# One scratch layout, one load for a part, new places, x in pieces and gram on 128 tokens in a convolution, FFT and MLP kernel

## The chip, the cores and the metric

The kernel runs on one core of a Trainium2 chip. The metric is the device time of one execution in microseconds (us), the median of several. A core has TensorE (PE, matrix products), VectorE (DVE), ScalarE (ACT), GpSimd (POOL) and SyncE (SP, which issues nearly all DMA transfers here), each with an instruction stream of its own. They meet at semaphores only. Sixteen DMA engines move data between HBM and the on-chip memory (SBUF, 128 partitions).

## The reference

`x` has the shape (32, 96, 56, 56): 32 images, 96 channels, 3,136 positions. Layer 0 is a ternary inverted residual block with batch statistics, layer 1 a token mixer with an FFT over the positions and an MLP with 8-bit operands:

```python
# layer 0; planes = 576
out = relu(batchnorm(conv(x, ternarize(w1)), g1, b1))
out = relu(batchnorm(conv(out, ternarize(w2), stride=1, pad=1, groups=planes), g2, b2))
out = batchnorm(conv(out, ternarize(w3)), g3, b3)
x = out + x
# layer 1; t is x as (image, position, channel)
t = t + attn(_ln_t(t)); t = t + ffn(_ln_t(t))

def attn(x):
    h = relu(_bn(einsum('bnc,hc->bnh', x, w1), ...))        # 192 hidden
    X = fft(h, axis=1, norm='ortho')
    xr = relu(X.real * rd - X.imag * idg + rb)
    xi = relu(X.imag * rd + X.real * idg + ib)
    y = ifft(xr + 1j * xi, axis=1, norm='ortho').real
    return _bn(einsum('bnh,ch->bnc', y, w2), ...)
def ffn(x):                                                 # fp8e5 operands, 384 hidden
    return _qlinear(relu(_qlinear(x, W1, b1)), W2, b2)
```

The mean and variance of the first batchnorm are over all images and positions, so nothing of the second convolution can start before all of `x` has been read once.

## The kernel before, in words

The program has four stages, one behind the other.

**Gram** (about 12 to 264 us). The statistics of the first batchnorm come from the products of `x` with itself over the positions. SP loads one image a transfer into one of two buffers (`xa`, L435). TensorE transposes blocks of `TP` = 112 positions (L458), ScalarE copies four of them from PSUM to `xT` (L494), and TensorE multiplies each by itself and sums into `gps` (L464): 28 blocks an image, in 7 groups of 4. Four transposes of one group and four products of the group before alternate.

**Convolution** (280 to 1880 us). `conv_sync`, `conv1_tensor` and their like run 16 image pairs, each with 18 steps `v` (two images, nine slices of channels). TensorE makes the 1x1 convolution (L651) and the depthwise one as products with diagonal taps (L683). SP stores four pieces of the result `z` a step (L618). At `v` = 1 and 8 it loads a whole image of the next pair into `xin` (L629), 96 partitions x 3,136; ScalarE and GpSimd split it into two 16-bit parts (`xhi_scalar`, L192, and L201).

**Projection** (1880 to 2553 us). `z` comes back in eighths of a pair, is normalised, and is multiplied by the third weight (L966). The result goes to `z_scratch` in halves (`store_half`). SP's part of it ends with a wait for the last stores.

**Tokens** (2553 to 5093 us). `tokens_stage` is a software pipeline over 32 images. A table `PLACES` gives each step one or more places on a line; `NT` = 2000 places are one turn, and a step placed at s belongs to turn position s mod 2000 for the image that started s div 2000 turns earlier. So up to `LAGS` = 5 images are in work, and each engine issues in the order of the places. There is no other order: an engine that waits holds all that stands behind it in its stream. The steps of one image:
- `load_in` (L1229, L1230) brings chunk c of the layer-0 result (`zin`) and of `x` (`x_tok`), seven chunks of 448 positions in three buffers; `act_bn3` (L1617) and `pool_y` (L1661) add them to `y`, `store_t` keeps a copy. With chunks 3 and 6 of image 0 the tables `t1c`, `g2c`, `g3c`, `t4c` are loaded (`load_tables`).
- `mean1` (L1336), `square1` (L1342) give the statistics of the first layer norm; a load `y<-va` (L1252) puts a row of `y` back.
- `w1` (L1474) and `stage1` (L1485) are the first linear map and the first stage of the FFT. `act_a` (L1605) writes a seventh of the result `a`, 128 partitions x 768, and `store_a` (L1287) stores it: seven stores an image, on the semaphores `st_a[p]`.
- `load_b` (L1263) brings the same data back the other way round as `bt`: 112 partitions (4 x 28) by frequency k, in four parts of 8, 8, 8 and 5 frequencies, each part with four transfers. The first part waits for all seven stores.
- `spectrum` (`bank_x`, L1418 and L1421), the scaling by the diagonals, `w2` (L1430, L1433), `stage3` (L1440 and `wz`), a scratch turn through `c_scratch` (`store_c`, `load_d`), and `stage4` (`bank_o<-t4c,d`, L1452), which adds to `tb` (`dve_residual`, L1767).
- The second layer norm (L1358, L1371 for the spreading of mean and inverse deviation), `mlp1` (L1400) and `mlp2` (`bank_o<-hq,fq`, L1463), and `store_out`.

The fourfold split of `load_b` comes from the layout of the scratch, in which partition 32q + k of `a` is row 32q + k:

```python
for q in range(4):
    src = a_d[f, 32 * q + k0:32 * q + k0 + n].rearrange("k j c -> j k c")
    sp.dma_start(bt[NJ * q:NJ * q + NJ, k0:k0 + n, :], src).then_inc(ld_b[k], 16)
```

Of the kernel before, what the change touches and what calls it, by code (L numbers as in the profile page):

```python
# [106 lines left out]
def build(nc, x4, cw1, g1, b1, cw2, g2, b2, cw3, g3, b3, aw1, bn1g, bn1b, bn1m, bn1v, ar, ai, arb, aib,  # L107
# [9 lines left out]
    a_d = nc.dram_tensor("a_scratch", (NB, 128, NJ, H), F32, kind="Internal").ap()  # L117
# [3 lines left out]
    with keep:  # L121
# [92 lines left out]
        with st:  # L214
# [196 lines left out]
            tps = [st.enter_context(nc.psum_tensor(f"tps{k}", [TP, 4, 128], F32)) for k in range(2)]  # L411
# [15 lines left out]
            NG = NJ // 4  # L427
# [60 lines left out]
            def gram_scalar(act, i):  # L488
                for m in range(2):
                    for g in range(NG):  # L490
# [3 lines left out]
                        nc.scalar.activation(xT[:, g % 2, :, 0:C], tps[g % 2][:, :, 0:C], ACT.Copy).then_inc(copied, 1)  # L494
# [1398 lines left out]
```

## Time and profile before

| | us |
|---|---|
| median of 3 executions (5085.65 to 5097.47) | 5097.38 |
| the profiled execution | 5094.76 |
| its span, first to last instruction | 5092.8 |
| PE busy | 4692.9 (92%) |
| DVE busy | 3398.0 (67%) |
| ACT busy | 3389.3 (67%) |
| POOL busy | 2513.4 (49%) |

The profile is of one execution. Its rows give when an instruction started, how long it ran, and what ended the idle time before it. The granted clock is that of TensorE as a share of its full 2.4 GHz. The DMA share is the mean busy share of the sixteen DMA engines. In a row such as `bank_x<-g2c,bt` the left name is written and the right ones are read. A transfer's landing is the time from its issue until its semaphore is complete.

### The profile page before, as it was taken

The page shows a single profiled execution, that of the slowest core. Times are in us where ns is not written, and L with a number is a line of the kernel's source. Part 1 is how long each engine was busy: PE and PEld are TensorE (multiplying, and loading weights), DVE is VectorE, ACT ScalarE, POOL GpSimd, SP SyncE. Part 2 cuts the span into 40 slices and gives each one's busy share as a digit, 9 for nine tenths or more (in the row PEclk, how much of TensorE's full clock was granted, in tenths as well). Part 3 has the DMA queues.
Part 4 walks back from the last instruction along what each step waited for, and adds up shares of the span by engine and source line. Part 5 has one row for each costly group of instructions (what it writes and reads, how often), then busy time and mean ns, then how long its engine had stood idle before and what let it go on. Part 6 is the DMA issues. An engine that isn't in the chain of part 4 may idle for free.

```text
span 5092.8 us, 151731 instructions
## 1 busy us (share of the span) xinstructions
PE 4692.9 (92%) x62292; PEld 3120.1 (61%) x62292; DVE 3398.0 (67%) x6475; ACT 3389.3 (67%) x5511; POOL 2513.4 (49%) x1508
## 2 busy tenths in 40 slices
PE   8989999999999989999948999999999999999986
PEld 8955555555555544444436666666666666666663
DVE  1156776677677865777715767777777776777676
ACT  4455665656566558888736777777777777777763
POOL 0067777777777755666613433343334334333431
PEclk9999999999999999999959999999999999999997
DMA  7657767776777779999947777777777767777762
GB/s 163 158 146 182 193 179 181 184 194 178 188 189 185 179 202 414 416 418 414 380 130 185 202 192 198 193 194 199 197 200 186 204 189 192 200 199 198 184 171 62
DMA packets 499822, 1072.01 MB, mean 210 GB/s; under 512 B 176608, under 2 KB 324608, under 8 KB 466240
## 3 DMA queue, kind: packets, MB, share of 16 engines
q1 hardware_dynamic: 499136, 1062.31, 72.5%
q8 instruction: 498, 8.16, 0.7%
q14 instruction: 188, 1.54, 0.1%
HBM read 557.40 MB, written 484.44 MB: 205 GB/s over the span
## 4 chain that ended last, share of the span: by engine, by line
PE 32%; DMA 8%; DVE 5%; issue 2%; ACT 1%; SPq 1%; POOL 1%; DVEq 0%; POOLq 0%; ACTq 0%
PE bank_w_s L1474 6%; PE bank_o L1452 4%; PE bank_x L1421 4%; DMA bt<-a_scratch 3%; PE bank_w_s L1485 3%; PE bank_c L1440 2%; PE bank_c L1433 2%; PE bank_c L1430 2%; DMA a_scratch<-a 2%; PE bank_l L1400 2%; PE bank_l L1342 2%; DMA tb<-t_scratch 1%; PE bank_x L1418 1%; PE bank_l L1358 1%; PE bank_l L1371 1%
## 5 line engine op out<-in xcount | busy, mean ns | idle before, releaser
L772 POOL TENSOR_TENSOR hlo<-h,hhi 128x1682 f16<-128x1682 f32 x288 | 977.6, 3394 | 377.8 <-DVE hhi L825 377.8
L735 ACT ACTIVATE h<-c1ps,s 128x1568 f32<-128x1568 f32 x288 | 479.3, 1664 | 625.4 <-PE c1ps L651 625.4
L785 DVE BATCH_NORM_STATS2 stats<-z 128x6 f32<-128x392 f32 x1152 | 597.1, 560 | 436.6 <-ACT z L725 426.4
L683 PE MATMUL dwps<-hhi,taps 64*64 64x392 f16 x13824 | 691.2, 330 | 12.6 <-issue 12.6
L683 PE MATMUL dwps<-hlo,taps 64*64 64x392 f16 x13824 | 683.6, 328 | 6.0 <-issue 6.0
L1668 POOL TENSOR_TENSOR s_plus<-d_minus,imag_scaled 128x448 f32<-128x448 f32 (+1 forms) x192 | 213.5, 1112 | 708.9 <-ACT imag_scaled L1535 708.9
L930 ACT ACTIVATE z2m<-z2m,s 128x784 f32<-128x784 f32 x512 | 489.6, 1029 | 105.2 <-DMA z2m<-z_scratch 104.8
L1677 POOL TENSOR_TENSOR onat<-tb,o 96x448 f32<-96x448 f32 x224 | 236.4, 1062 | 620.8 <-DVE o L1737 620.8
L954 POOL TENSOR_TENSOR h_split<-z2m,h_split 128x1568 f16<-128x1568 f32 x128 | 405.3, 3166 | 266.6 <-DVE h_split L993 266.6
L683 PEld LDWEIGHTS dwps<-hhi,taps 64*64 64x64 f16 x13824 | 380.6, 106 | 253.3 <-issue 107.0
L683 PEld LDWEIGHTS dwps<-hlo,taps 64*64 64x64 f16 x13824 | 405.0, 106 | 187.3 <-issue 8.4
L1611 ACT ACTIVATE h<-bank_w_s,rt 128x192 f32<-128x192 f32 x896 | 318.9, 421 | 207.9 <-DVE rt L1743 207.6
L1661 POOL TENSOR_TENSOR y<-zin,x_tok 96x448 f32<-96x448 f32 x224 | 254.5, 1149 | 313.8 <-ACT zin L1617 313.6
L1550 ACT ACTIVATE h<-bank_l 128x448 f16<-128x448 f32 x672 | 342.8, 543 | 77.4 <-PE bank_l L1400 65.4
L1474 PE MATMUL bank_w_s<-w1a,y 97*128 97x193 f32 x1792 | 372.3, 344 | 16.0 <-DMA y<-va 8.4
L966 PE MATMUL pps<-z2m,w3T 128*96 128x392 f32 x1024 | 361.4, 496 | 15.1 <-ACT z2m L930 15.1
L201 POOL TENSOR_TENSOR xlo<-xin,x_packed 96x448 f16<-96x448 f32 x224 | 233.8, 1045 | 285.2 <-ACT x_packed L192 285.1
L1474 PEld LDWEIGHTS bank_w_s<-w1a,y 97*128 97x128 f32 x1792 | 308.5, 197 | 53.6 <-issue 20.2
L1767 DVE SCALAR_TENSOR_TENSOR tb<-bank_o,w2shift,tb 96x448 f32<-96x448 f32 x224 | 152.3, 680 | 251.4 <-PE bank_o L1452 211.7
L825 DVE CAST hhi<-h 128x1682 f16<-128x1682 f32 x288 | 297.7, 1034 | 9.0 <-ACT h L740 9.0
L1452 PE MATMUL bank_o<-t4c,d 128*96 128x112 f32 x1792 | 224.9, 270 | 64.7 <-DVE tb L1767 57.2
L1421 PE MATMUL bank_x<-g2c,bt 112*128 112x112 f32 x1856 | 244.1, 285 | 41.8 <-DMA bt<-a_scratch 35.5
(234 smaller groups left out, 9673.0 us busy)
## 6 DMA issues: line engine op xcount, KB each, us to landing
z_scratch<-z SPq DMA_DIRECT2D x1152, 196.0 KB, 3.3
z2m<-z_scratch SPq DMA_DIRECT2D x64, 1960.0 KB, 15.8
z2m<-z_scratch SPq DMA_DIRECT2D x64, 1568.0 KB, 11.5
a_scratch<-a SPq DMA_DIRECT2D x224, 384.0 KB, 3.9
bt<-a_scratch SPq DMA_DIRECT2D x384, 168.0 KB
t_scratch<-y SPq DMA_DIRECT2D x32, 1344.0 KB, 8.9
c_scratch<-cc SPq DMA_DIRECT2D x128, 336.0 KB, 3.8
d<-c_scratch SPq DMA_DIRECT2D x128, 336.0 KB, 4.7
```

Source lines behind the costliest of these rows:

```text
L683: ins = nc.tensor.matmul(dw[64 * j:64 * j + 64, r, g, 0:QN], taps[half, u, da, dx, :, :].rearrange("p y c -> p (y c)"), part[half, s, a0:a ...
L735: nc.scalar.activation(to, src, ACT.Relu, bias=s1[:, 1, u:u + 1], scale=s1[:, 0, u:u + 1]).then_inc(h_ready, 1)
L772: nc.gpsimd.tensor_tensor(to, h, hi, ALU.subtract).then_inc(lo_ready, 1)
L785: nc.vector.bn_stats(stats[:, i, v, at:at + 6], z2[:, v % 3, g, r, :]).then_inc(s_stat, 1)
L930: nc.scalar.activation(v, v, ACT.Relu, bias=s2[:, 1, t:t + 1], scale=s2[:, 0, t:t + 1]).then_inc(h2_ready, 1)
L954: nc.gpsimd.tensor_tensor(lo, h32, hi, ALU.subtract).then_inc(lo_ready, 1)
L966: nc.tensor.matmul(banks[m], w3T[:, t, :], z2m[:, c // 2, 4 * m + t, cols], start=(t == 0), stop=False)
L1421: ins = nc.tensor.matmul(xs[:, s, 0:TP], bt[:, k0 + s, 0:128], g2c[:, :], start=True, stop=True)
L1452: ins = nc.tensor.matmul(OB[0:C, 0, k * TP:k * TP + TP], d[:, j, :], t4c[:, j, :], start=True, stop=True)
L1474: ins = nc.tensor.matmul(WS[:, g % 2, e * (H + 1):(e + 1) * (H + 1)], both, w1a[:, :], start=True, stop=True)
L1550: nc.scalar.activation(h16[:, c % 2, q, :], LL[k % 2][:, 0, 0:CH], ACT.Copy).then_inc(h16_done, 1)
L1611: nc.scalar.activation(h[:, g % 2, e * H:e * H + H], WS[:, g % 2, e * (H + 1):e * (H + 1) + H], ACT.Relu, scale=rt[:, g % 2, e, :]).then_i ...
```

## The change

1. **Scratch of `a` by frequency.** `a_scratch` is laid out (image, 32, 4, NJ, H) instead of (image, 128, NJ, H): frequency first, then the quarter q. A part of `load_b` is one transfer over 112 partitions, and the waits on `ld_b` count 16 a part, not 64. `store_a` writes the same 128 partitions x 768 to a target that is walked as q, k, (j c).
2. **New places** for every step of the token stage. Two lines of the table are shown.
3. **x in pieces.** In the convolution the next pair's images come in seven pieces of 96 x 448 each, at the steps `v` = 1 to 14, on the same semaphore; the consumer waits for all seven.
4. **Gram on 128 positions.** 24 blocks of 128 and one of 64 an image, 25 instead of 28, still in 7 groups.
5. **First chunks ahead.** `zin`, `x_tok` and `ld_in` live from the start. SP issues chunks 0 to 2 of image 0 at the end of the projection, once the first of the last stores are in, and `load_in` leaves them out. The table `t1c` is loaded with the others behind chunk 6.

```diff
-    a_d = nc.dram_tensor("a_scratch", (NB, 128, NJ, H), F32, kind="Internal").ap()
+    a_d = nc.dram_tensor("a_scratch", (NB, 32, 4, NJ, H), F32, kind="Internal").ap()
...
+        zin = sb("zin", [C, 3, CH])
+        x_tok = sb("x_tok", [C, 3, CH])
+        ld_in = [sem(f"loaded_in{k}") for k in range(3)]
...
         def xhi_scalar(act, j, m, c):
             if c == 0:
-                act.wait_ge(ldx[m], j * 16 + 16)
+                act.wait_ge(ldx[m], j * 16 * NCH + 16)
...
-            NG = NJ // 4
+            NG = -(-TOK // 512)
+
+            def blocks_of(g):
+                return [(at, min(128, TOK - at)) for at in range(512 * g, min(512 * g + 512, TOK), 128)]
...
-                            for k in range(4):
-                                at = (4 * g + k) * TP
-                                ins = nc.tensor.transpose(tps[g % 2][:, k, 0:C], xa[:, m, at:at + TP], ident[0:C, 0:C])
+                            for k, (at, p) in enumerate(blocks_of(g)):
+                                ins = nc.tensor.transpose(tps[g % 2][0:p, k, 0:C], xa[:, m, at:at + p], ident[0:C, 0:C])
                             ins.then_inc(turned, 1)
                         if g >= 1:
                             pe.wait_ge(copied, n + g)
-                            for k in range(4):
+                            for k, (at, p) in enumerate(blocks_of(g - 1)):
                                 b = (g - 1) % 2
-                                ins = nc.tensor.matmul(gps[m][:, 0:C + 1], xT[:, b, k, 0:C], xT[:, b, k, :],
+                                ins = nc.tensor.matmul(gps[m][:, 0:C + 1], xT[0:p, b, k, 0:C], xT[0:p, b, k, :],
                                                        start=(i == 0 and g == 1 and k == 0),
-                                                       stop=(i == NP - 1 and g == NG and k == 3))
+                                                       stop=(i == NP - 1 and at + p == TOK))
...
-                    if more and v in (1, 8):
-                        m = v // 8
-                        sp.wait_ge(xlo_ready, (2 * i + m + 1) * (NCH + 1))
-                        sp.dma_start(xin[:, m, :], x[2 * i + 2 + m]).then_inc(ldx[m], 16)
+                    if more and 1 <= v <= 2 * NCH:
+                        m, c = divmod(v - 1, NCH)
+                        if c == 0:
+                            sp.wait_ge(xlo_ready, (2 * i + m + 1) * (NCH + 1))
+                        cols = slice(c * CH, c * CH + CH)
+                        sp.dma_start(xin[:, m, cols], x[2 * i + 2 + m, :, cols]).then_inc(ldx[m], 16)
...
+                for h in range(2):
+                    sp.wait_ge(stz[h], 32)
                 store_half(sp, NP - 1, 1)
+                for c in range(3):
+                    cols = slice(c * CH, c * CH + CH)
+                    sp.dma_start(zin[:, c, :], z3_d[0, :, cols]).then_inc(ld_in[c], 16)
+                    sp.dma_start(x_tok[:, c, :], x[0, :, cols]).then_inc(ld_in[c], 16)
...
- 'store_a': (2915, 3059, 3270, 3379, 3518, 3605, 3666),
- 'load_b': (3871, 4014, 4834, 5012),
+ 'store_a': (3658, 3970, 4101, 4265, 4423, 4518, 4550),
+ 'load_b': (4644, 4838, 5619, 5748),
...
     def load_in(sp, n, c):
+        if isinstance(n, int) and n == 0 and c < 3:
+            return
...
     def load_tables(sp, c):
-        if c == 3:
+        if c == 6:
             sp.dma_start(t1c[:, :, :], t1_d.rearrange("p (j c) -> p j c", j=NJ)).then_inc(s_t1, 16)
-        if c == 6:
...
         k0, n = K_OF[k]
-        for q in range(4):
-            src = a_d[f, 32 * q + k0:32 * q + k0 + n].rearrange("k j c -> j k c")
-            sp.dma_start(bt[NJ * q:NJ * q + NJ, k0:k0 + n, :], src).then_inc(ld_b[k], 16)
+        src = a_d[f, k0:k0 + n].rearrange("k q j c -> (q j) k c")
+        sp.dma_start(bt[:, k0:k0 + n, :], src).then_inc(ld_b[k], 16)
...
         v = a[:, (par + p) % 2, :, :].rearrange("p b x -> p (b x)")
-        sp.dma_start(a_d[f, :, 4 * p:4 * p + 4, :].rearrange("p j c -> p (j c)"), v).then_inc(st_a[p], 16)
+        to = a_d[f, :, :, 4 * p:4 * p + 4, :].rearrange("k q j c -> q k (j c)")
+        sp.dma_start(to, v).then_inc(st_a[p], 16)
```

What the new order looks like on the engines, at three places. First SP's stream in a turn of the token stage, from the last stores of `a` to the first two parts of `bt`; before:

```order
L1287 DMA a_scratch<-a 128x768
L1298 DMA out_dram<-onat 96x3136
L1287 DMA a_scratch<-a 128x768
L1268 DMA c_scratch<-cc 112x8x96
L1287 DMA a_scratch<-a 128x768
L1275 DMA d<-c_scratch 32x2688
L1287 DMA a_scratch<-a 128x768
L1282 DMA tb<-t_scratch 96x512
L1263 DMA bt<-a_scratch 28x8x192 x4
L1282 DMA tb<-t_scratch 96x512 x2
L1263 DMA bt<-a_scratch 28x8x192 x4
L1229 DMA zin<-z_scratch 96x448
```

and after the change:

```order
L1300 DMA a_scratch<-a 4x32x768
L1306 DMA t_scratch<-y 96x3584
L1300 DMA a_scratch<-a 4x32x768
L1280 DMA c_scratch<-cc 112x8x96
L1243 DMA zin<-z_scratch 96x448
L1244 DMA x_tok<-in_x_dram 96x448
L1300 DMA a_scratch<-a 4x32x768 x2
L1287 DMA d<-c_scratch 32x2688
L1294 DMA tb<-t_scratch 96x512
L1275 DMA bt<-a_scratch 112x8x192 x2
L1280 DMA c_scratch<-cc 112x8x96
L1294 DMA tb<-t_scratch 96x512 x2
```

Each part is one row of 112 partitions where it was four of 28, and a store's target is 4x32x768 where it was 128x768.

Second, TensorE late in a turn, up to the first spectrum product of the next image (`bank_x`, the last row); before:

```order
L1463 MATMUL bank_o<-hq,fq 96x448 x3
L1430 MATMUL bank_c<-w2q,zq 112x192 x2
L1433 MATMUL bank_c<-w2p,zp 112x96 x4
L1400 MATMUL bank_l<-yq,fq 128x448 x3
L1440 MATMUL bank_c<-wz,g3c 112x384
L1400 MATMUL bank_l<-yq,fq 128x448 x2
L1463 MATMUL bank_o<-hq,fq 96x448 x3
L1400 MATMUL bank_l<-yq,fq 128x448
L1430 MATMUL bank_c<-w2q,zq 112x192 x2
L1433 MATMUL bank_c<-w2p,zp 112x96 x4
L1371 MATMUL bank_l<-mean_parts,sel 96x224 x2
L1421 MATMUL bank_x<-g2c,bt 128x112 x8
```

and after:

```order
L1413 MATMUL bank_l<-yq,fq 128x448 x2
L1476 MATMUL bank_o<-hq,fq 96x448 x3
L1453 MATMUL bank_c<-wz,g3c 112x384
L1413 MATMUL bank_l<-yq,fq 128x448 x2
L1476 MATMUL bank_o<-hq,fq 96x448 x3
L1443 MATMUL bank_c<-w2q,zq 112x192 x2
L1446 MATMUL bank_c<-w2p,zp 112x96 x4
L1413 MATMUL bank_l<-yq,fq 128x448 x2
L1476 MATMUL bank_o<-hq,fq 96x448 x3
L1453 MATMUL bank_c<-wz,g3c 112x384
L1384 MATMUL bank_l<-mean_parts,sel 96x224 x2
L1434 MATMUL bank_x<-g2c,bt 128x112 x8
```

One more group of `bank_o<-hq,fq` and a `bank_c<-wz,g3c` stand close before the spectrum product; the single `bank_l<-yq,fq` rows have moved.

Third, SP in the convolution, around the load of one image for the next pair; before:

```order
L211 DMA x_low_rest<-xlo 64x1568
L618 DMA z_scratch<-z 32x2x784 x12
L629 DMA xin<-in_x_dram 96x3136
L618 DMA z_scratch<-z 32x2x784 x24
L209 DMA x_packed<-xlo 32x3192
L210 DMA x_low_rest<-xlo 64x1624
L211 DMA x_low_rest<-xlo 64x1568
```

and after:

```order
L625 DMA z_scratch<-z 32x2x784 x12
L638 DMA xin<-in_x_dram 96x448
L625 DMA z_scratch<-z 32x2x784 x4
L638 DMA xin<-in_x_dram 96x448
L625 DMA z_scratch<-z 32x2x784 x4
L638 DMA xin<-in_x_dram 96x448
L625 DMA z_scratch<-z 32x2x784 x4
L638 DMA xin<-in_x_dram 96x448
L625 DMA z_scratch<-z 32x2x784 x4
```

The one transfer of 96x3136 has become seven of 96x448 with four stores of `z` between each two.

## Rows read from the trace of the kernel before

**Rows 1.** The page's first line
```profile
span 5092.8 us, 151731 instructions
```

**Rows 2.** Windows: us, busy by engine, granted clock, DMA share, GB/s
```profile
12.00:264.00 252.00, 243.09 (x2712) 234.93 (x2712) 38.93 (x112) 109.47 (x231) 1.06 (x2) 1.00 0.70 160
...
280.00:1880.00 1600.00, 1565.60 (x36864) 920.43 (x36864) 1154.02 (x1756) 954.07 (x1400) 1203.60 (x536) 0.99 0.71 182
1880.00:2553.00 673.00, 636.58 (x2560) 312.35 (x2560) 462.69 (x659) 546.30 (x577) 405.26 (x128) 0.98 0.98 401
...
3307.00:4406.00 1099.00, 1012.37 (x9321) 749.12 (x9322) 794.30 (x1804) 819.58 (x1522) 417.99 (x387) 0.99 0.74 196
```

**Rows 3.** Chain of waits around one `bt` load: start, us, what
```profile
3601.25 2.65 DMA a_scratch<-a
...
3605.42 4.80 DMA bt<-a_scratch
...
3610.27 1.81 PE bank_x L1421 x14
```

**Rows 4.** Chain of waits, the same place in two turns
```profile
2870.99 2.04 PE bank_x L1421 x16
...
4944.11 2.04 PE bank_x L1421 x16
```

**Rows 5.** Timeline of TensorE in gram: start, us, instruction
```profile
164.74 0.49 PE L458 MATMUL tps<-ident,xa 96*112 96x96 f32 x4
...
165.75 0.41 PE L458 MATMUL tps<-ident,xa 96*112 96x96 f32 x3
```

**Rows 6.** Tile `xa`: its loads
```profile
DMA to landing us min/median/max: 7.0/7.5/12.5
```

**Rows 7.** Timeline of SP, first and last load before a stop
```profile
328.25 0.47 SPq L629 DMA_DIRECT2D xin<-in_x_dram  x1
...
1721.16 0.43 SPq L629 DMA_DIRECT2D xin<-in_x_dram  x1
```

**Rows 8.** Timeline of TensorE, first and last of twelve; [idle before <-reason]
```profile
338.81 1.20 PE L683 MATMUL dwps<-hlo,taps 64*64 64x392 f16 x23 [1.59 <-issue]
...
1731.00 0.53 PE L683 MATMUL dwps<-hhi,taps 64*64 64x392 f16 x6 [1.82 <-issue]
```

**Rows 9.** Windows, 10 us behind the first of these loads
```profile
328.00:338.00 10.00, 8.82 (x205) 4.68 (x197) 7.54 (x12) 5.33 (x8) 6.26 (x3) 1.00 0.88 257
```

**Rows 10.** Chain of waits, first and seventh chunk of the token stage
```profile
2567.82 3.18 DMA x_tok<-in_x_dram
...
2578.34 6.66 DMA x_tok<-in_x_dram
```

**Rows 11.** What TensorE waited for, 3307 to 4406: us, times, longest
```profile
PE bank_o L1452 <- DVE tb L1767: 26.2, 30, 1.7
PE bank_x L1421 <- DMA bt<-a_scratch: 12.7, 15, 1.7
```

**Rows 12.** Timeline of TensorE late in a turn
```profile
3686.33 0.90 PE L1440 MATMUL bank_c<-wz,g3c 112*112 112x384 f32 x2
3687.06 0.73 PE L1463 MATMUL bank_o<-hq,fq 128*96 128x448 fp8e5 x3
```

**Rows 13.** DMA: 2613.5-2616.2 (one store, two lines), 2649.5-2653 (`bt`), 2671.4-2673.5 (`va`)
```profile
DMA packets 144, 0.39 MB, mean 146 GB/s; under 512 B 16, under 2 KB 16, under 8 KB 144
...
q1 hardware_dynamic: 144, 0.39, 37.4%
...
DMA packets 962, 0.70 MB, mean 199 GB/s; under 512 B 56, under 2 KB 962, under 8 KB 962
...
DMA packets 16, 0.01 MB, mean 4 GB/s; under 512 B 8, under 2 KB 16, under 8 KB 16
```

**Rows 14.** Windows with TensorE's granted clock (seventh number)
```profile
2670.00:2675.00 5.00, 1.88 (x16) 1.70 (x16) 1.42 (x4) 2.99 (x5) 0.84 (x1) 1.00 0.07 13
2675.00:2680.00 5.00, 5.00 (x36) 4.62 (x34) 2.09 (x5) 2.11 (x5) 1.70 (x3) 0.66 0.99 215
```

More of the change, by code:

```diff
@@ L410, in build @@
             gtmp = [sb(f"gtmp{k}", [128, UN], ctx=st) for k in range(4)]
-            tps = [st.enter_context(nc.psum_tensor(f"tps{k}", [TP, 4, 128], F32)) for k in range(2)]
+            tps = [st.enter_context(nc.psum_tensor(f"tps{k}", [128, 4, 128], F32)) for k in range(2)]
             gps = [st.enter_context(nc.psum_tensor(f"gps{k}", [C, 512], F32)) for k in range(2)]
@@ L493, in gram_scalar @@
                         wait_count(act, xt_used, n - 1)
-                        nc.scalar.activation(xT[:, g % 2, :, 0:C], tps[g % 2][:, :, 0:C], ACT.Copy).then_inc(copied, 1)
+                        blocks = blocks_of(g)
+                        p, k = blocks[0][1], len(blocks)
+                        nc.scalar.activation(xT[0:p, g % 2, 0:k, 0:C], tps[g % 2][0:p, 0:k, 0:C], ACT.Copy).then_inc(copied, 1)
             @block.scalar
@@ new lines @@
+PLACES = {'load_in': (449, 1615, 1618, 1699, 1728, 1749, 2084),
+ 'act_bn3': (1595, 1688, 1700, 1950, 2093, 2163, 2214),
+ 'pool_y': (1502, 1606, 1628, 1708, 1922, 2121, 2277),
+ 'store_t': (2272,),
+ 'act_square1': (2816, 3271),
+ 'mean1': (3411,),
+ 'square1': (3411, 3432),
+ 'act_mean1': (3259,),
+ 'dve_var1': (3444,),
+ 'act_std1': (3390,),
+ 'row1': (3603,),
+ 'w1': (3522, 3533, 3700, 3732, 3815, 3821, 3925, 3960, 4188, 4327, 4457, 4470, 4564, 4653),
+ 'dve_rstd1': (3622, 3653, 3775, 3803, 4015, 4034, 4140, 4155, 4246, 4287, 4359, 4399, 4492, 4540),
+ 'act_h': (3513, 3586, 3707, 3711, 3905, 3914, 4161, 4163, 4297, 4355, 4521, 4524, 4644, 4653),
+ 'stage1': (3603, 3798, 3894, 4026, 4437, 4500, 4724),
+ 'act_a': (3674, 3842, 4038, 4169, 4509, 4531, 4769),
+ 'store_a': (3658, 3970, 4101, 4265, 4423, 4518, 4550),
+ 'load_b': (4644, 4838, 5619, 5748),
+ 'spectrum': (5187, 5419, 5497, 5757, 5907, 6453),
+ 'act_scaled': (5064, 5384, 5470, 5845, 6147, 6530),
+ 'dve_real': (5311, 5511, 5727, 6108, 6288, 6506),
+ 'pool_imag': (4917, 5290, 5379, 5659, 6000, 6651),
+ 'act_relu': (5177, 5396, 5629, 6034, 6384, 6799),
+ 'dve_fold': (5434, 5559, 5869, 6224, 6423, 6795),
+ 'w2': (5573, 5814, 5963, 6354, 6711, 6822, 7019, 7208),
+ 'dve_wz': (5765, 6027, 6210, 6355, 6601, 6795, 6928, 7144),
+ 'stage3': (5693, 5852, 6259, 6548, 6763, 6935, 7120, 7255),
+ 'dve_c': (5859, 6110, 6258, 6470, 6708, 6834, 6976, 7144),
+ 'store_c': (5793, 6444, 6863, 7068),
+ 'load_d': (6209, 6566, 7072, 7345),
+ 'load_t': (6582, 6883, 6912, 7080, 7432, 7511, 7675),
+ 'stage4': (7435, 7440, 7518, 7561, 7577, 7676, 7710),
+ 'dve_residual': (7462, 7535, 7595, 7698, 7741, 7773, 7842),
+ 'act_square2': (7704, 7786),
+ 'mean2': (7639, 7780),
+ 'square2': (7769, 7814),
+ 'act_mean2': (7797,),
+ 'dve_var2': (8012,),
+ 'dve_mparts': (7874,),
+ 'act_std2': (7888,),
+ 'dve_rstd2': (8138,),
+ 'spread_mean': (7825, 8412, 8732, 9162),
+ 'spread_rstd': (7992, 8482, 8821, 9213),
+ 'dve_centre': (8163, 8184, 8351, 8352, 8649, 8685, 8987),
+ 'dve_norm': (8201, 8206, 8406, 8419, 8730, 8746, 9242),
+ 'mlp1': (8177, 8182, 8207, 8237, 8333, 8347, 8514, 8557, 8585, 8652, 8693, 8717, 8827, 8872, 8939, 8968, 9062, 9073,
+          9330, 9338, 9380),
+ 'act_h16': (8196, 8203, 8216, 8297, 8313, 8319, 8545, 8575, 8612, 8620, 8677, 8695, 8830, 8863, 8894, 8904, 8935,
+             8939, 9133, 9143, 9174),
+ 'dve_bias1': (8244, 8251, 8286, 8297, 8335, 8371, 8489, 8499, 8511, 8550, 8723, 8815, 8840, 8841, 8863, 8959, 9043,
+               9049, 9316, 9327, 9367),
+ 'dve_relu1': (8289, 8446, 8574, 8819, 8901, 9097, 9400),
+ 'mlp2': (8494, 8766, 8873, 8998, 9120, 9385, 9427),
+ 'act_o': (8578, 8804, 8880, 8933, 8986, 9199, 9349),
+ 'dve_bias2': (8570, 8889, 8933, 9081, 9258, 9382, 9620),
+ 'pool_out': (8405, 8697, 8740, 8778, 8926, 9016, 9450),
+ 'store_out': (9750,)}
@@ L1153, in tokens_stage @@
     s_t1, s_g, s_t4 = sem("t1_loaded"), sem("g2_g3_loaded"), sem("t4_loaded")
-    ld_in = [sem(f"loaded_in{k}") for k in range(3)]
     bn3_done, y_done, st_t = sem("bn3_done"), sem("y_done"), sem("t_stored")
```

67 lines of the change are left out of this document (5 added, 62 removed).

## Prediction

> **What bounds the kernel now.** I read the span first: 5092.8 us [rows 1]. The profiled execution took 5094.76 us, 2.6 us under the median of 5097.38, so the sum below is made against 5094.8. Next I read the busy time by stretch [rows 2]. TensorE is busy 243 of 252 us in the gram stretch, 1566 of 1600 in the convolution, 637 of 673 in the projection (there the DMA share is 0.98 at 401 GB/s) and 1012 of 1099 in the middle of the token stage, where the DMA share is 0.74. So the kernel is TensorE-bound nearly everywhere, and a gain must take away matmuls or TensorE's waits. Last I read the chain of waits. It passes through one place of every turn of the token stage, from a scratch store to the load of `bt` to the first spectrum product [rows 3]. Two passages of that place, 28 turns apart, give the turn: (4944.11 − 2870.99) / 28 = 74.04 us [rows 4]. There are 32 images, so one microsecond per turn is 32 us.
>
> **Gram on 128 tokens.** Four transposes and their four products take 165.75 − 164.74 = 1.01 us [rows 5], or 0.2525 us a block. An image has 25 blocks instead of 28, which is 0.76 us less. Its period is 252 / 32 = 7.88 us [rows 2], so TensorE alone would go to 7.12 us and the stage would lose 24 us. The load of the next image but one is issued once its buffer is free, and lands after 7.0 us at least, 7.5 at the median and 12.5 at most [rows 6]; it has one period and about half a microsecond of products to do it in. That is enough at the median and not in the slower ones, so I keep three quarters: **−18 us** (−6 to −24).
>
> **x in seven pieces (convolution).** TensorE stands still for reasons that the profile calls "issue" some 10 us after a whole-image load: the first is issued at 328.25 and TensorE stands for the 1.59 us before 338.81; the last one at 1721.16, with 1.82 us before 1731.00 [rows 7, 8]. There are twelve such stops over 0.8 us, 20.9 us in all. In the 10 us behind the issue the DMA share is 0.88 at 257 GB/s against 0.71 at 182 in the stage [rows 2, 9], so whatever TensorE's sequencer fetches then stands behind 1.2 MB. A piece is a seventh of it, with four z stores between pieces, so two thirds of these stops should go: **−14 us** (0 to −21). SP issues 12 more transfers a pair, but it isn't on TensorE's path. The Trainium skill (DMA: Bandwidth & Descriptors, Measured) speaks against this part: it asks for transfers of at least 1 MiB for three quarters of the peak rate. By that rule the stage would not gain; here 0.71 of the engines' time suffices, so the rule would only turn −14 into 0.
>
> **First chunks ahead, table later (start of the token stage).** The first chunk's wait of 3.18 us goes [rows 10]. The seventh chunk's load took 6.66 us because the load of the table `t1c` (`load_tables` at chunk 3) stood before it [rows 10]; at the first chunk's 3.18 it saves 3.5 us. Together **−7 us** (−4 to −9). `t1c` is needed only after the normalisation, much later.
>
> **New places, one load for a part.** The visible waits which the new order could remove are bank_o on `tb` (26.2 us over 1099 us, some 1.8 us a turn) and bank_x on `bt` (12.7 us, 0.86 a turn) [rows 11]. The stage-4 products no longer stand in one block of twelve, and two more groups of `hq` products and one of `wz` now stand between the last stage-1 product and spectrum[0]. A `wz` group takes the engine 3687.06 − 3686.33 = 0.73 us; one of `hq` is busy for 0.73, some 0.6 of it alone [rows 12]; together 1.9. One load for four saves three issues, 1.2 us, in the same path. Against it, the last six products of w2, stage 3 and `c` now run up to the end of the turn with less beside them: w2[7], stage3[7], the norm, mlp1[18] and mean1 follow one another there. I count those at what the removed waits gave, 1.5 to 2.5 us. **Net 0**, with bounds from −1.5 to +2 us a turn (−48 to +64).
>
> **The store of `a`.** This decides it. The store used to have 128 rows of 3,072 bytes on both sides. Its target is now 4 x 32 x 768: the slowest dimension is 4. How many DMA engines share a transfer can be read from its small closing packets. One store of 128 rows leaves 16 of them among 144 packets; four `bt` loads of 28 rows leave 56, 14 each; the loads of `va` with four runs leave 8 for two, 4 each [rows 13]. In each case the count is the largest number up to 16 that divides the leading size. If 4 leads, the store runs on 4 engines. None of these rows has 128 on one side and 4 on the other, so that 4 wins is an inference. The Trainium skill (DMA: Bandwidth & Descriptors, Why a DMA increments its semaphore by 16 and not by 1) states it: the number must divide both patterns' slowest dimension. By that rule, the trace agrees for 128, 28 and 4.
>
> The cost: the window with one store holds 37.4% of 2.7 us on each engine [rows 13], 1.01 us for 8 packets, so 0.126 us a packet. On 4 engines each carries 32 packets, 4.0 us. A store that landed after 2.65 us [rows 3] would take 2.65 + 3.0 = 5.7. In a turn each engine is now busy 0.74 x 74.04 = 54.8 us, of which 7 stores are 7.1. The other twelve go to 47.7. The four go to 47.7 + 7 x 4.04 = **76.0 us in a turn of 74**. They are full. The highest share that any stretch shows is 0.98 [rows 2], which gives a turn of at least 77.6 us, +3.5.
>
> The wait is worse than the mean says, since the stores stand in one part of the turn: by the new places 3658 to 4550 of 2000 a turn, six steps of 149, or 5.5 us each. In that time one of the four gets 4.04 + 47.7 / 74 x 5.5 = 7.6 us of work; its queue grows by 2.1 a store, to 12.5 by the seventh. `load_b` waits for all seven, SP stands on it with the loads of `d`, `tb` and x behind, and spectrum[0] waits for that load. From the store to the product it is now 3610.27 − 3601.25, that is 2.65 + 1.5 of issues + 4.80 = 8.97 us [rows 3], of which 0.86 is wait, so 8.1 us are covered, and 10.0 with the 1.9 us of new products. It becomes 5.7 + 0.3 + 4.8 + the backlog = 10.8 + backlog, so late by 0.8 plus the backlog. As TensorE then idles, a turn leaves more time to drain, so I take 8.5 for the backlog, between 2 and 12. After such an idle time TensorE's clock falls: behind 5 us with 1.88 us of work its mean is 0.66 over the next 5 [rows 14], part at 1.2 and part at 2.4 GHz, which costs 1.7. Sum **+11 us a turn**, bounds +3.5 and +17; 32 x 11 = **+352**.
>
> **Sum.** 5094.8 − 18 − 14 − 7 + 0 + 352 = 5408, rounded 5405. Without the store's part it is 5056.
>
> **Rivals.**
> A. The store still spreads over 16 engines, because the 128 partitions of the source set the number. For it: nothing in the trace contradicts it directly. Against: each row where a count can be read follows the leading size on the memory side. Result 5056; with the order between −0.7 and +2 us a turn it is 5034 to 5120. Chance 0.15; it is also the case in which the change does what it says.
> B. The four engines carry it but only the mean binds: the backlog drains beside other work, and the turn goes to 77 to 78. For it: the new order leaves 1.9 us more before spectrum[0], and fewer issues. Against: the stores lie within 892 of the turn's 2000 places. Result 5056 + 32 x 3 = 5152. Chance 0.08.
> C. As A, and the order removes 1.5 us of waits a turn: 5056 − 48 = 5008. Chance 0.04.
> A and C end on the other side of the time before; what divides them from the forecast is one number, on how many engines 393 KB of `a` lie: they are full where 7 x 1.01 x 16 / n + 47.7 exceeds 74, that is from n = 4 down.
>
> **How the numbers follow.** Forecast 0.73, its own range 5210 to 5600 (+3.5 and +17 us a turn, less or more the other terms). The range is 5050 to 5590: below it lie C and a third of A, 0.09, above it 0.04 of the forecast's tail. A measurement of this kernel tells 0.3% (15 us) from no change. Faster holds C and A without A's upper edge: 0.16. Within 0.3%: that edge, 0.03. Slower: the forecast and B, 0.81.
>
> **What would show it.** The store's landing, 2.65 us before, at 5 us or more, with 4 small packets and 32 packets on each of four engines; the DMA share of the token stage falling as the turn grows past 77; bank_x waiting on `bt<-a_scratch` for some 9 us a turn and a lower granted clock behind it. In the convolution the stops on "issue" fall from twelve to about four; the gram stretch lasts 234 us. If the store lands in under 3 us with 16 closing packets, the forecast is wrong and rival A holds. If it lands late and the turn grows by 3 us at most, B holds and the backlog was the step that failed.

## The result and the profile after

The changed kernel takes 5719.16 us (median of 4, 5714.88 to 5725.64) against 5097.43 us: a ratio of 1.121, interval 1.119 to 1.123. It is slower, as forecast, but by 622 us where I had 310, and it lies outside the range of 5050 to 5590.

The page of the changed kernel: span, busy time with its share, the DMA queue of the data, and the chain that ended last by engine.

```profile
span 5723.7 us, 150952 instructions
...
PE 4964.7 (87%) x62004; PEld 3285.8 (57%) x62004; DVE 3455.4 (60%) x6475; ACT 3373.0 (59%) x5511; POOL 2601.9 (45%) x1508
...
q1 hardware_dynamic: 511488, 1062.29, 62.9%
...
PE 28%; DMA 20%; DVE 3%; ACT 2%; issue 2%; SPq 1%; POOL 0%; DVEq 0%; POOLq 0%; ACTq 0%
```

The bytes are those of before, and their share of the sixteen engines falls from 72.5% to 62.9%: the data moves no faster, the kernel is longer. The chain now holds 20% of DMA, where it held 8%.

Where the stages begin can be read from the first start of three groups: the first convolution product, the first projection product, and the first and last spectrum product. Before:

```profile
L651 PE MATMUL c1ps<-x_packed,t1h x4608: 329/329/534, 280.1 to 1865.3; 128*32 128x392 f16 x192
...
L966 PE MATMUL pps<-z2m,w3T x1024: 492/492/937, 1897.8 to 2553.0; 128*96 128x392 f32 x171
...
L1421 PE MATMUL bank_x<-g2c,bt x1856: 261/275/523, 2653.9 to 4990.4; 112*128 112x112 f32 x186
```

and after the change:

```profile
L660 PE MATMUL c1ps<-x_packed,t1h x4608: 329/329/534, 265.5 to 1821.0; 128*32 128x392 f16 x192
...
L981 PE MATMUL pps<-z2m,w3T x1024: 492/492/969, 1853.5 to 2506.0; 128*96 128x392 f32 x171
...
L1434 PE MATMUL bank_x<-g2c,bt x1856: 261/275/556, 2604.7 to 5624.9; 112*128 112x112 f32 x186
```

| | before | after | difference |
|---|---|---|---|
| first convolution product | 280.1 | 265.5 | −14.6 (gram) |
| from it to the first projection product | 1617.7 | 1588.0 | −29.7 (convolution) |
| from it to the last projection product of this kind | 655.2 | 652.5 | −2.7 |
| from it to the first spectrum product | 100.9 | 98.7 | −2.2 (start of the token stage) |
| first to last spectrum product | 2336.5 | 3020.2 | **+683.7** |
| from there to the end of the span | 102.4 | 98.8 | −3.6 |

The sum is 630.9 us, which is the difference of the spans. All that was lost lies in the turns: 683.7 us over the 31 from the first to the last image are 22.1 us each. (The row also holds the spectrum products of the last image; a turn in the middle grew by 21.3 us, as the next rows show.)

Twelve turns of either kernel, before and after, in windows (length, busy time of PE, PEld, DVE, ACT and POOL, granted clock, DMA share, GB/s):

```profile
3312.90:4201.40 888.50, 818.49 (x7534) 605.43 (x7533) 642.93 (x1462) 663.58 (x1235) 335.80 (x312) 0.99 0.74 196
```

```profile
3735.90:4879.50 1143.60, 918.17 (x7456) 669.84 (x7457) 657.54 (x1438) 652.87 (x1221) 361.62 (x307) 0.85 0.53 150
```

A turn is 95.3 us long in that stretch and 74.0 before. In it TensorE's granted clock is 0.85, where it was 0.99. TensorE is busy 918.17 / 12 = 76.5 us of a turn and waits 18.8; before it was busy 818.49 / 12 = 68.2 us and waited 5.8. What TensorE waited for in the window after the change (us in total, times, longest):

```profile
PE bank_x L1434 <- DMA bt<-a_scratch: 87.4, 12, 8.3
PE bank_l L1371 <- DVE tb L1780: 52.2, 12, 4.5
PE bank_w_s L1487 <- ACT a L1618: 39.9, 12, 4.0
PE bank_l L1413 <- DVE yq L1770: 19.1, 24, 1.0
```

Per turn that is 7.3 us on `bt`, 4.4 on `tb`, 3.3 on `a` and 1.6 on `yq`. The chain of waits shows where the first and third come from (start, us, what):

```profile
3599.42 9.62 DMA a_scratch<-a
...
3619.33 9.42 DMA a_scratch<-a
...
3629.67 10.68 DMA a_scratch<-a
...
3640.58 5.01 DMA bt<-a_scratch
...
3645.63 3.76 PE bank_x L1434 x16
```

These stores of `a` land after 9.62, 9.42 and 10.68 us; the last one before the load took 2.65 [rows 3]. The chain passes the last two in a row, joined by ScalarE's copy to `a`. The load behind them takes 5.01 us, as before, and the sixteen spectrum products behind that take 3.76 us instead of 2.04 [rows 4]: the same work at the lower clock.

### The profile page after: what moved, and what is told of

The parts are those of the page before. It is cut to its first block, busy times and chain, and to the rows that moved or that the text cites. A ratio compares the mean times of both kernels' runs of the same rounds, so it can differ in the third digit from the quotient of the medians.

```text
span 5723.7 us, 150952 instructions
## 1 busy us (share of the span) xinstructions
PE 4964.7 (87%) x62004; PEld 3285.8 (57%) x62004; DVE 3455.4 (60%) x6475; ACT 3373.0 (59%) x5511; POOL 2601.9 (45%) x1508
## 3 DMA queue, kind: packets, MB, share of 16 engines
q1 hardware_dynamic: 511488, 1062.29, 62.9%
## 4 chain that ended last, share of the span: by engine, by line
PE 28%; DMA 20%; DVE 3%; ACT 2%; issue 2%; SPq 1%; POOL 0%; DVEq 0%; POOLq 0%; ACTq 0%
DMA a_scratch<-a 12%; DMA tb<-t_scratch 5%; PE bank_w_s L1487 4%; PE bank_x L1434 4%; DMA bt<-a_scratch 3%; PE bank_w_s L1498 3%; PE bank_c L1443 2%; PE bank_c L1446 2%; PE bank_o L1465 2%; PE bank_l L1413 2%; PE bank_l L1355 2%; PE bank_l L1349 2%; ACT a L1618 2%; PE bank_o L1476 1%; PE bank_c L1453 1%
## 5 line engine op out<-in xcount | busy, mean ns | idle before, releaser
L1690 POOL TENSOR_TENSOR onat<-tb,o 96x448 f32<-96x448 f32 x224 | 327.4, 1462 | 791.2 <-DVE o L1750 791.2
L945 ACT ACTIVATE z2m<-z2m,s 128x784 f32<-128x784 f32 x512 | 489.9, 1029 | 102.6 <-DMA z2m<-z_scratch 102.4
L1487 PE MATMUL bank_w_s<-w1a,y 97*128 97x193 f32 x1792 | 413.3, 371 | 112.2 <-ACT a L1618 105.9
L1434 PE MATMUL bank_x<-g2c,bt 112*128 112x112 f32 x1856 | 292.4, 322 | 241.8 <-DMA bt<-a_scratch 231.5
L1487 PEld LDWEIGHTS bank_w_s<-w1a,y 97*128 97x128 f32 x1792 | 338.2, 216 | 179.7 <-ACT a L1618 140.5
L1434 PEld LDWEIGHTS bank_x<-g2c,bt 112*128 112x128 f32 x1856 | 273.0, 232 | 263.7 <-DMA bt<-a_scratch 223.3
L1544 ACT ACTIVATE d_minus<-bank_x,diag 128x448 f32<-128x448 f32 (+1 forms) x192 | 132.2, 689 | 419.6 <-PE bank_x L1434 376.4
L981 PE MATMUL pps<-z2m,w3T 128*96 128x392 f32 x1024 | 362.3, 497 | 15.5 <-ACT z2m L945 15.5
```

The source lines that it names most:

```text
L945: nc.scalar.activation(v, v, ACT.Relu, bias=s2[:, 1, t:t + 1], scale=s2[:, 0, t:t + 1]).then_inc(h2_ready, 1)
L981: nc.tensor.matmul(banks[m], w3T[:, t, :], z2m[:, c // 2, 4 * m + t, cols], start=(t == 0), stop=False)
L1434: ins = nc.tensor.matmul(xs[:, s, 0:TP], bt[:, k0 + s, 0:128], g2c[:, :], start=True, stop=True)
L1487: ins = nc.tensor.matmul(WS[:, g % 2, e * (H + 1):(e + 1) * (H + 1)], both, w1a[:, :], start=True, stop=True)
L1690: nc.gpsimd.tensor_tensor(to, v, o, ALU.add).then_inc(out_done, 1)
```

## Experiments

The table has the kernels that were run. Its last column is the time from the first to the last spectrum product, read from the same row as above, so it leaves the stages ahead out. The median is of the kernel's runs. The ratio, with its 95% interval, is to runs of the kernel before made at the same time (medians 5095 to 5110), so it isn't exactly the quotient of two rows.

| kernel | median us | ratio | spectrum, first to last |
|---|---|---|---|
| before | 5097 | 1 | 2336.5 |
| the change | 5719 | 1.121 (1.119 to 1.123) | 3020.2 |
| after_store4 | 5058 | 0.992 (0.990 to 0.994) | 2356.5 |
| after_old_layout | 5027 | 0.986 (0.984 to 0.988) | 2327.1 |
| before_pad4 | 5605 | 1.099 (1.096 to 1.102) | 2843.2 |
| before_pad8 | 5435 | 1.066 (1.062 to 1.069) | 2675.0 |
| after_a3 | 5722 | 1.121 (1.117 to 1.125) | 3022.1 |
| after_old_places | 5532 | 1.084 (1.080 to 1.088) | 2818.3 |
| stages_only | 5047 | 0.989 (0.986 to 0.992) | 2344.1 |
| before_x_pieces | 5068 | 0.993 (0.990 to 0.995) | 2336.3 |
| after_tb_first | 5487 | 1.077 (1.074 to 1.080) | 2780.2 |
| old_layout_tb_first | 5024 | 0.987 (0.984 to 0.990) | 2312.8 |

### after_store4: the same bytes in four transfers of 32 rows

```diff
-        to = a_d[f, :, :, 4 * p:4 * p + 4, :].rearrange("k q j c -> q k (j c)")
-        sp.dma_start(to, v).then_inc(st_a[p], 16)
+        for q in range(4):
+            to = a_d[f, :, q, 4 * p:4 * p + 4, :].rearrange("k j c -> k (j c)")
+            sp.dma_start(to, v[32 * q:32 * q + 32, :]).then_inc(st_a[p], 16)
```

The waits on `st_a` count 64 instead of 16.

> The changed kernel with each store of a issued as four transfers of 32 rows (one per quarter q, the same bytes to the same addresses). A target of 32 rows can spread over 16 engines. Theory T (the store on 4 DMA engines costs everything that was lost): the 4.0 to 7.5 us of a store's transfer go back to about 1 us, the turn goes from about 95.3 us to 74 (72 to 76), and the total to 5720 - 31 x 22 = about 5040 us (4990 to 5100). Rival P (the new places, or bt as one transfer, cost by themselves): turn stays at 78 us or more, total above 5160 us. The 21 more issues a turn cost SP about 21 x 0.35 = 7 us of a turn in which it has room.

5058 us, 661 us less than the change. The addresses, the places and the single load of a part are those of the change; only the shape of the store differs. So the shape of the store carries the whole loss (T), and P falls.

### after_old_layout: layout, store and loads as before, all else changed

```diff
-        to = a_d[f, :, :, 4 * p:4 * p + 4, :].rearrange("k q j c -> q k (j c)")
-        sp.dma_start(to, v).then_inc(st_a[p], 16)
+        sp.dma_start(a_d[f, :, 4 * p:4 * p + 4, :].rearrange("p j c -> p (j c)"), v).then_inc(st_a[p], 16)
```

(with `a_d` as (NB, 128, NJ, H), and `load_b` in four transfers, as before)

> The changed kernel with the scratch layout, the store of a (128 rows of 768) and the load of a part (four transfers of 28 rows) as before; places, pieces of x, gram and first chunks stay as changed. Theory T: total 5000 to 5100 us, near the run with four stores of 32 rows; the difference between the two is what one transfer for four loads is worth, at most 1.2 us a turn, 40 us. Rival P with the new places as the cause: above 5160 us here as well.

5027 us. Here is the chain of waits at the same place of a turn as shown above:

```profile
3687.98 2.71 DMA a_scratch<-a
3692.21 5.19 DMA bt<-a_scratch
3697.44 2.04 PE bank_x L1434 x16
```

The store takes 2.71 us and the load 5.19. This kernel beats both given ones, and it is 31 us faster than after_store4. So 21 more store transfers a turn, together with the other scratch layout, cost more than single loads give; the two weren't separated. With the stores spread, the whole change without its first part is worth 70 us.

### before_pad4 and before_pad8: the number of engines alone

```diff
-    a_d = nc.dram_tensor("a_scratch", (NB, 128, NJ, H), F32, kind="Internal").ap()
+    a_d = nc.dram_tensor("a_scratch", (NB, 4, 33, NJ, H), F32, kind="Internal").ap()
...
-            src = a_d[f, 32 * q + k0:32 * q + k0 + n].rearrange("k j c -> j k c")
+            src = a_d[f, q, k0:k0 + n].rearrange("k j c -> j k c")
...
-        sp.dma_start(a_d[f, :, 4 * p:4 * p + 4, :].rearrange("p j c -> p (j c)"), v).then_inc(st_a[p], 16)
+        to = a_d[f, :, 0:32, 4 * p:4 * p + 4, :].rearrange("q k j c -> q k (j c)")
+        sp.dma_start(to, v).then_inc(st_a[p], 16)
```

before_pad8 does the same with (NB, 8, 17, NJ, H) and 16 rows a group.

> The kernel before with one edit: its scratch gets a row of padding behind every 32, so that a store's target is 4 x 32 x 768 and not 128 x 768, while rows stay 21.5 KB apart and loads and places are those of before. Theory T (number of engines): the store lands after 9 us or more, the turn goes to 90 us or more, total 5600 to 5900 us. Rival L (the new memory layout with rows 86 KB apart is what makes the store slow): no change, 5097 +- 15 us, landing 2.3 to 4 us.

> The kernel before with a row of padding behind every 16 of its scratch: the store's target is 8 x 16 x 768. By the count of closing packets it should use 8 engines, 16 packets on each. Busy time on these eight: 47.7 + 7 x 2.0 = 61.8 us of a 74 us turn, so they don't fill. If only full engines cost time: 5097 +- 15 us. If a later landing costs as well (double buffer of a, load of bt behind the last store): one to three us a turn, 5130 to 5200 us. Theory T expects the second, far less than half of what 4 engines cost.

The padded row is the only thing that differs from the kernel before: +507 us in the turns, with the old places, the old loads and rows 21.5 KB apart. Rival L falls. The chain of before_pad4:

```profile
3629.27 8.24 DMA a_scratch<-a
...
3639.80 4.66 DMA bt<-a_scratch
```

With 8 engines the count can be read once more. This is a window of 5.5 us with one store in it, from the first turn, where no other transfer runs:

```profile
DMA packets 136, 0.39 MB, mean 71 GB/s; under 512 B 8, under 2 KB 8, under 8 KB 136
...
q1 hardware_dynamic: 136, 0.39, 29.9%
```

136 packets, of which 8 are closing ones: 8 engines, the divisor of 8 and 128. The next store lands after 5.32 us. In the middle turns the chain passes two stores, and they land later (the first is issued right behind the store of `y`, the second is the last before the load of `bt`):

```profile
2650.39 5.32 DMA a_scratch<-a
...
3637.63 11.41 DMA a_scratch<-a
...
3664.16 6.29 DMA a_scratch<-a
```

It costs +338 us in the turns, 10.9 us a turn, and my expectation there was 1 to 3. From 3353.43 to 4713.31 us there are sixteen turns of 85.0 us, with TensorE busy 1173.56 us at a granted clock of 0.92. So of the 10.9 us a turn, 5.8 are added waits and 5.1 are more time for the same products.

The window shows one more thing, which my expectation had wrong. 29.9% of 5.5 us on sixteen engines is 1.64 us; on the eight that carry the store it is 3.3 us, or 0.206 for each of 16 packets, not 0.126. With four engines it is similar. In before_pad4 only stores of `a` run from 2634 to 2641 us:

```profile
q1 hardware_dynamic: 149, 0.44, 23.0%
```

If all of it lies on four engines, each is busy 6.4 of the 7 us. Six of the 149 packets are closing ones, so that is some 36 full packets on each, 0.18 us a packet and 5.8 us a store. The same reading in the changed kernel (2591.3 to 2598.9 us, 187 packets, 7 of them closing, 21.5%) gives 0.15 and 4.7 us. So the packets of a narrow store took longer than those of a wide one. Eight engines are then busy not 61.8 us of 74 but 47.7 + 7 x 3.3 = 70.8, an estimate that spreads all else evenly: still not full in the mean, but close to it. That stores queue on them in the part of the turn where they lie can't be excluded.

### after_a3: a third buffer of `a`

```diff
-    a = sb("a", [128, 2, 2, 2 * H])
+    a = sb("a", [128, 3, 2, 2 * H])
...
-        if p >= 2:
-            act.wait_ge(st_a[p - 2], f * 16 + 16)
-        else:
-            wait_count(act, st_a[p + 5], f * 16)
-        nc.scalar.activation(a[:, (par + p) % 2, :, :], WS[:, :, 0:2 * H], ACT.Copy).then_inc(a_done, 1)
+        if p >= 3:
+            act.wait_ge(st_a[p - 3], f * 16 + 16)
+        else:
+            wait_count(act, st_a[(6, 4, 5)[p]], f * 16)
+        nc.scalar.activation(a[:, p % 3, :, :], WS[:, :, 0:2 * H], ACT.Copy).then_inc(a_done, 1)
```

> The changed kernel with three buffers of a instead of two (slot p % 3; ScalarE waits for the store three back, or for st_a[6], [4], [5] of the image before): stores still run on 4 DMA engines. Theory B (the double buffer of a holds the stage-1 products back, since a store lands after 9.5 us): the wait of bank_w_s on ScalarE's a, 3.3 us a turn, goes, and part of the clock loss with it: 5720 - 31 x (3 to 7) = 5500 to 5630 us. Rival Q (the stores themselves queue on the four engines, so the last of the seven lands as late as before whatever the buffers): the wait moves to bank_x on bt; total within 1% of 5720 us.

5722 us, no change (Q). What TensorE waited for from 3400 to 4900 us, first in the change, then with three buffers:

```profile
PE bank_x L1434 <- DMA bt<-a_scratch: 114.7, 16, 8.3
PE bank_l L1371 <- DVE tb L1780: 65.4, 15, 4.6
PE bank_w_s L1487 <- ACT a L1618: 53.2, 16, 4.0
```

```profile
PE bank_x L1434 <- DMA bt<-a_scratch: 109.4, 15, 10.4
PE bank_l L1371 <- DVE tb L1780: 69.9, 16, 4.9
PE bank_l L1413 <- ACT h L1563: 31.4, 31, 3.1
```

The 53.2 us on `a` are gone, and 31.4 us on ScalarE's `h` of the MLP stand there instead; the waits on `bt` and `tb` stay. The double buffer is a place at which the late stores are seen; taking it away gave no time.

### after_old_places: the old order under late stores

The table `PLACES` of the kernel before, in the changed kernel; nothing else.

> The changed kernel with the places of before: scratch by frequency, store on 4 engines, one load a part, pieces of x, gram and first chunks as changed. The padded version of before took +509 us with the same places. If the two layouts cost alike: 5604 - 47 (what the stages ahead of the tokens gained) = about 5560 us, less up to 40 us for single loads. If the new places cost more under late stores than the old ones, this run is below 5650 us and the rest up to 5720 is theirs; if rows 86 KB apart are slower than rows 21.5 KB apart, it is at 5720 us or above.

5532 us, 187 us less than the change. In the turns it is 25 us below before_pad4 (2818.3 against 2843.2), which is 0.8 us a turn for single loads and the other layout together. So nothing shows that rows 86 KB apart are slower than rows 21.5 KB apart. And the new places, worth 17 us with spread stores (2344.1 in stages_only, 2327.1 in after_old_layout), cost 202 with late ones.

### after_tb_first and old_layout_tb_first: what stands behind a store

The load of `tb` explains it. The chain of the changed kernel, where a turn's first store is issued:

```profile
3672.99 0.59 SPq L1300
...
3673.71 9.19 DMA tb<-t_scratch
3682.92 0.69 DVE tb L1780
...
3683.66 1.24 PE bank_l L1371 x12
```

SP issues the store at 3672.99 and the seventh load of `tb` at 3673.71. The load takes 9.19 us; with it `tb`'s addition and the mean of the second layer norm are late, and TensorE waits over 4 us. In the old order that load stood elsewhere. One number was moved:

```diff
- 'load_t': (6582, 6883, 6912, 7080, 7432, 7511, 7675),
+ 'load_t': (6582, 6883, 6912, 7080, 7432, 7511, 7650),
```

> The changed kernel with one number moved: the seventh load of tb (load_t) at place 7650 instead of 7675, so that SP issues it just before the first store of a and not just behind it. In the changed kernel that load took 9.19 us behind a store on 4 engines, and TensorE waited up to 4.6 us for it (65.4 us in 1500). Theory F (what is queued behind such a store lands as late as the store does): the load lands in about 5 us, the 4.3 us of TensorE's wait go, 31 x 4.3 = 133 us less, and a little more by the clock: 5560 to 5620 us. Rival: the chain through the stores of a sets the turn and the 4 us reappear at its waits: above 5680 us.

> The same number moved in the kernel with the changed stages and places but the scratch layout, store and loads of before (5027 us). There a store takes 1.1 us of 16 engines, so by theory F the order of the two transfers is worth nothing: 5027 +- 10 us. If the move is a gain of the order by itself, it comes here too, and this is then the fastest version.

5487 us: 232 us less, for two neighbouring transfers that change places. F holds in its direction and in where the wait was; the size is 7.7 us a turn where 4.3 was expected. Much of the rest is time of the products themselves: from 3323.28 to 4736.14 us there are sixteen turns of 88.3 us, in which TensorE is busy 1182.96 us. That is 14.4 us of waits and 73.9 of work a turn, 4.4 and 2.6 less than in the change. The wait on `tb` at L1371 is no longer among those of TensorE, the others remain at their size:

```profile
PE bank_x L1434 <- DMA bt<-a_scratch: 119.0, 17, 7.7
PE bank_w_s L1487 <- ACT a L1618: 56.9, 17, 3.8
```

(17 turns in 1500 us.) In the kernel with spread stores the same move is worth nothing that can be told, 5024 us (5011 to 5037) against 5027. So the order was no worse by itself; it had put a load right behind a transfer that takes 9 us where it used to take 3. With the move the new places are no longer behind the old ones under late stores (2780.2 against 2818.3), so this one neighbourhood accounts for all of the 202 us.

### stages_only and before_x_pieces: the parts ahead of the tokens

stages_only is after_old_layout with the old `PLACES`. before_x_pieces is the kernel before with the seven loads of x at `v` = 1 to 14, and the wait on all seven.

```diff
-                    if more and v in (1, 8):
-                        m = v // 8
-                        sp.wait_ge(xlo_ready, (2 * i + m + 1) * (NCH + 1))
-                        sp.dma_start(xin[:, m, :], x[2 * i + 2 + m]).then_inc(ldx[m], 16)
+                    if more and 1 <= v <= 2 * NCH:
+                        m, c = divmod(v - 1, NCH)
+                        if c == 0:
+                            sp.wait_ge(xlo_ready, (2 * i + m + 1) * (NCH + 1))
+                        cols = slice(c * CH, c * CH + CH)
+                        sp.dma_start(xin[:, m, cols], x[2 * i + 2 + m, :, cols]).then_inc(ldx[m], 16)
```

> The kernel before with the gram blocks of 128, x in pieces and the first chunks ahead only; the token stage with its scratch and its places as before. By the trace of the changed kernel the token stage starts 47 us earlier: 5096 - 47 = about 5049 us (5035 to 5060). My prediction had 39 us for these three. The difference to the run with the old layout and the new places (5027 us) is what the places are worth: about 20 us.

> The kernel before with x loaded in seven pieces in the convolution, nothing else. If the pieces end TensorE's stops on issue and nothing else in that stage changes: -20 to -30 us, 5066 to 5076 us. If the 29.7 us by which the stage got shorter come from something else (gram's end, a lower load on the queue at its start): less than -10 us.

stages_only took 5047 us, before_x_pieces 5068. In the latter the first projection product starts at 1868.3 instead of 1897.8:

```profile
L968 PE MATMUL pps<-z2m,w3T x1024: 492/492/967, 1868.3 to 2522.9; 128*96 128x392 f32 x171
```

That is 29.5 of the 29.7 us of the convolution stage, with the pieces alone. Before, TensorE waited on "issue" for 18.6 us in the depthwise products (`dwps`) and 4.1 in the 1x1 ones (`c1ps`). In the changed kernel this is left of them:

```profile
PE dwps L692 <- issue: 0.3, 1, 0.3
```

## Why the prediction was wrong, step by step

- **The store runs on 4 engines.** Right. The inference that 4 wins over 128 is borne out by 8 closing packets for 8 rows against 128, and by before_pad4, where 16 closing packets stand among 472 while only stores of `a` run, some three and a half of them (2631.5 to 2653.9 us). The Trainium skill (DMA: Bandwidth & Descriptors, Why a DMA increments its semaphore by 16 and not by 1) has this rule; the runs with 8 and 4 agree with it.
- **Its landing.** 5.7 us forecast for a store alone; 9.62 measured for one issued 22 us behind the store before it, though right behind a store of 336 KB. In the fill of the token stage one landed after 7.5 us in the change (2591.26), and one after 5.32 on eight engines. The price of a packet was the wrong step here: 0.126 us was read from a store on 16 engines, and on 4 it is 0.15 to 0.18, so 4.7 to 5.8 us a store and not 4.0. The backlog of 8.5 us, on the other hand, did not come at that size: the last store of the turn lands after 10.68 us, where 5.7 + 8.5 = 14.2 was forecast.
- **What it holds up.** I priced one wait, spectrum[0] on `bt`, at 8.5 + 0.8 us a turn. It came to 7.3 us, of which 0.86 had been there before and was not taken off in my sum. From that store to the product it took 16.0 us instead of 19.3, but only 8.7 of them were covered, where I had 10.0. But I left out two others: ScalarE's copy into the double buffer of `a`, of which the working says nothing (3.3 us of TensorE a turn), and the load of `tb` behind the first store (4.4 us). The prediction says that SP stands with the loads of `d`, `tb` and x behind it, and then prices nothing of it. TensorE's waits went from 5.8 to 18.8 us a turn: +13.0 instead of +9.3. These two waits, put at nothing, are the first step that failed.
- **The clock.** Forecast 1.7 us a turn, and this is the largest miss, the second step that failed. A turn has 95.3 − 18.8 = 76.5 us outside of waits, and had 74.0 − 5.8 = 68.2 for nearly the same products: +8.3. With the waits that makes the 21.3 us of a turn, where 11 were forecast. It recurs in two other kernels: +5.1 us of work with +5.8 of waits in before_pad8, −2.6 with −4.4 in after_tb_first. Three stretches of 10 us in a turn show it (granted clock is the figure before the last two):

```profile
3640.00:3650.00 10.00, 4.37 (x20) 4.24 (x20) 1.08 (x3) 0.57 (x1) 1.61 (x1) 0.66 0.87 218
3680.00:3690.00 10.00, 6.34 (x48) 3.78 (x49) 4.06 (x9) 4.84 (x8) 0.91 (x1) 0.71 0.65 225
3700.00:3710.00 10.00, 5.98 (x32) 4.16 (x31) 4.92 (x10) 4.41 (x9) 2.53 (x3) 0.73 0.41 138
```

TensorE stands still at three places of a turn, on `bt`, `tb` and `a`, and around each the granted clock is at 0.66 to 0.73 in the mean, between its levels of 1.2 and 2.4 GHz. I had taken one such place with its 1.7 us. At the first, the sixteen spectrum products alone lost 1.7 us.
- **The criterion.** "Full engines" was the point from which I let the forecast decide, with a lower bound of +3.5 us. before_pad8 costs 10.9 us a turn, and its eight engines are not full in the mean: at a DMA share of 0.68 in 85.0 us they carry, by my estimate, 57.8 − 11.6 + 23.1 = 69 us. So engines that aren't full do not make a late landing free. In before_pad4 the same estimate gives 86 of 90 us, and in the change some 75 of 95 (4.7 us a store), so nearly full engines remain a possible limit in the first and hardly in the second. Rival B, in which only the mean binds, gave a turn of 77 to 78 us; it was 95.3.
- **Gram on 128 tokens.** −18 forecast, −14.6 measured. Fewer blocks are less work, as I had it, but the load is not what takes the rest back: TensorE waits for it 1.2 us in all, 0.4 before. Its busy time falls by 15.5 us (243.09 from 12 to 264 us, 227.61 from 12 to 249.5), where I had 24; a product took 0.094 us in the mean instead of 0.090.
- **x in pieces.** −14 forecast with −21 as the bound, −29.7 measured. The stops on "issue" went altogether, not by two thirds. Beside them TensorE's busy time in the stage fell from 1566.0 to 1557.8 us, 8 us that I had not foreseen and can't explain. The Trainium skill's rule (DMA: Bandwidth & Descriptors, Measured) of 1 MiB a transfer did not bind.
- **First chunks ahead.** −7 forecast. With spread stores the time from the last projection product to the first spectrum product falls by 8.0 us (stages_only); in the change it is 5.8 longer than that. With the same new places and spread stores (after_old_layout) it is 92.6, close to the 92.9 of stages_only, so it is the late stores that take it back.
- **New places and single loads.** Net 0 (−48 to +64) forecast, −17 measured for the places with spread stores. Single loads, with the layout that they need, give 0.8 us a turn under late stores, where I had 1.2; they were not run with spread stores and nothing else.

The sum without the store's part was 5056, and the nearest run, after_store4, took 5058. That they agree so well is luck: x gave 16 us more than forecast, and after_store4 took 31 us more than the kernel with the old layout. The store's part was +352 and is +664 in the turns (3020.2 − 2356.5).

The range of the forecast has a slip of its own: +3.5 us a turn on 5056 is 5168, not 5210.

What stays open: why a packet of the same 3,072 bytes took 0.15 to 0.21 us in stores on 4 or 8 engines and 0.126 on 16, how much of the loss is queueing on these engines, and how much of the 8.3 us belongs to which of the three idle places. The clock wasn't varied by itself in any run.

## What to carry to other kernels

Before a scratch layout is changed to make one transfer of four on the load side, look at what the store's target becomes: with an outermost size of 4, 8 or 128 it ran on 4, 8 or 16 engines here, and seven slow stores cost more than single loads give. A transfer that lands late is paid where its landing is waited for and by what is issued right behind it, also where its engines are not full in the mean; so list every wait on its semaphore, the release of its source buffer too, and every transfer issued just behind it. And where TensorE is to idle anew, price the clock at each idle place, not once.

## What the runs showed of the hardware that I had not expected

- The last store of a turn, 393 KB in 128 rows, lands after 2.65 us on 16 engines, 6.29 on 8, and 8.24 (before_pad4) to 10.68 (the change) on 4.
- A packet of 3,072 bytes in such a store kept its engine for 0.126 us on 16 engines, 0.206 on 8, and 0.15 to 0.18 on 4 (estimates from the share of busy time).
- A load of 197 KB issued 0.7 us behind a store on 4 engines took 9.19 us. Issued just ahead of it instead, it no longer held TensorE up, and the kernel was 232 us faster.
- Waits of 13.0 us more in a turn went with 8.3 us more for the same products, at a granted clock of 0.85 instead of 0.99.
- With loads of 1.2 MB in the convolution the stage took 29.5 us longer than with the same bytes in seven pieces; 22.7 us of it are stops of TensorE that the profile calls "issue", and with the pieces 0.3 are left.
